# Nucleus step 0 with four threshold evaluations and a middle first point, open rows handled tile by tile, and the preparing stage folded into attention

## What is computed

```python
h = maximum(layernorm(x), 0)
x = x + L0(h, adj)        # eight-head graph attention, logits plus 2 * adj, zeros of adj masked
h = maximum(layernorm(x), 0)
x = x + L1(h, adj)        # diffusion and a nucleus-limited attention, two steps
...
# inside L1, for each of two steps:
logits = (Xa @ W1) @ W2 @ (Xa @ W3).T
vals = sort(logits, descending); csum = cumsum(softmax(vals))
k_i = sum(csum < 0.9) + 1                 # per row: smallest set of columns with 0.9 of the mass
A = softmax(where(rank < k_i, logits, -inf))
Xf = Rf @ Xf; Xb = Rb @ Xb; Xa = A @ Xa   # Rf, Rb: adj + 1 on the diagonal, divided by row or column sums
Z = Z + Xf @ U1[s] + Xb @ U2[s] + Xa @ U3[s]
```

## Time and profile before

| | us |
|---|---|
| median of three runs (3515.78 to 3516.79) | 3516.76 |
| the profiled execution | 3525.11 |
| its span, first to last instruction | 3523.3 |
| PE busy | 2934.2 |
| DVE busy | 2265.8 |
| ACT busy | 1292.9 |
| POOL busy | 50.1 |

### The profile page before, as it was taken

How to read it: one execution, slowest core, us unless ns; L and a number is a source line. 1 busy time by engine, 2 the same in 40 slices (tenths; PEclk the granted TensorE clock), 3 DMA queues, 4 the chain that set the end, 5 groups by cost and what they waited for, 6 DMA issues and landing times. The chain is left out here.

```text
span 3523.3 us, 57798 instructions
## 1 busy us (share of the span) xinstructions
PE 2934.2 (83%) x20374; PEld 2147.0 (61%) x20374; DVE 2265.8 (64%) x4452; ACT 1292.9 (37%) x1686; POOL 50.1 (1%) x68
## 2 busy tenths in 40 slices
PE   2469999999999999999999465887866568688599
PEld 1356666767667676676766244665645356577488
DVE  7955656556565655555556489789487987896430
ACT  4733434344334343434433221332414243422311
POOL 0000000000000000000000100000000000000110
PEclk7579999999999999999999787999988789899899
DMA  7937748386583865838568111101011000000500
GB/s 263 373 127 187 180 113 198 95 199 164 131 196 93 199 149 143 202 88 201 131 159 199 57 54 37 39 23 49 1 48 37 1 25 25 31 19 25 221 1 25
DMA packets 586123, 396.75 MB, mean 113 GB/s; under 512 B 538371, under 2 KB 551174, under 8 KB 560390
## 3 DMA queue, kind: packets, MB, share of 16 engines
q1 hardware_dynamic: 584262, 382.49, 39.8%
q10 hardware_dynamic: 1728, 12.58, 1.1%
HBM read 223.05 MB, written 37.75 MB: 74 GB/s over the span
## 5 line engine op out<-in xcount | busy, mean ns | idle before, releaser
L681 DVE SCALAR_TENSOR_TENSOR e_lo<-e,e_hi 128x2048 f16<-128x2048 f32 x128 | 293.3, 2291 | 448.1 <-ACT e_hi L606 448.1
L560 PE MATMUL av<-vw_hi,pT_hi 128*128 128x256 f16 x2048 | 559.4, 273 | 7.6 <-DMA pT_lo<-e_lo 7.6
L560 PE MATMUL av<-vw_lo,pT_hi 128*128 128x256 f16 x2048 | 559.4, 273 | 0.0
L560 PE MATMUL av<-vw_hi,pT_lo 128*128 128x256 f16 x2048 | 559.4, 273 | 0.0
L549 PE MATMUL logits<-kT_hi,qT_hi 128*128 128x512 f16 x1024 | 389.0, 380 | 7.2 <-DVE att_small L667 5.5
L1830 DVE SCALAR_TENSOR_TENSOR nuc_junk<-nuc_e,nuc_thr 128x2048 bf16<-128x2048 f32 x168 | 388.4, 2348 | 5.1 <-issue 0.5
L549 PE MATMUL logits<-kT_lo,qT_hi 128*128 128x512 f16 x1024 | 388.1, 379 | 0.0
L549 PE MATMUL logits<-kT_hi,qT_lo 128*128 128x512 f16 x1024 | 388.1, 379 | 0.0
L600 ACT ACTIVATE att_small<-att_small,minus 128x1 f32<-128x1 f32 x128 | 37.7, 295 | 829.2 <-DVE att_small L676 829.2
L667 DVE CUSTOM_DVE_ANT_0 e<-logits,bias,att_small 128x1024 f32<-128x1024 f32 x256 | 328.6, 1284 | 0.0
L601 ACT ACTIVATE e<-e,att_small,sc 128x2048 f32<-128x2048 f32 x128 | 266.2, 2079 | 0.0
(11 more groups left out here) (399 smaller groups left out, 5806.9 us busy)
## 6 DMA issues: line engine op xcount, KB each, us to landing
bias<-bias_scratch SPq DMA_DIRECT2D x130, 1024.0 KB, 4.8
bias_scratch<-adj_bias SPq DMA_DIRECT2D x16, 1024.0 KB, 8.0
adjT_scratch<-adjT SPq DMA_DIRECT2D x16, 1024.0 KB, 7.6
nuc_at_hi<-adjT_scratch SPq DMA_DIRECT2D x32, 512.0 KB, 3.9
nuc_at_lo<-adjT_scratch SPq DMA_DIRECT2D x32, 512.0 KB, 4.8
adjT<-adjT_scratch SPq DMA_DIRECT2D x16, 1024.0 KB, 19.5
adj_rows<-in_adj_dram ACTq DMA_DIRECT2D x12, 1024.0 KB, 9.2
adj_rows<-in_adj_dram SPq DMA_DIRECT2D x4, 1024.0 KB, 7.9
```

What stands on the lines that cost most here:

```text
L560: last = nc.tensor.matmul(AV[par][:, :], PT[par][w][:, m, :], VW[x][:, m, :], start=(m == 0 and w == x == 0), stop=(m == T - 1 and w == 1))
L681: nc.vector.scalar_tensor_tensor(out=EL[:, :], in0=E[par][:, :], scalar=P_SCALE, in1=EH[:, :], op0=ALU.mult, op1=ALU.subtract).then_inc(lo ...
```

## The change

- `CUTS` goes from (5, 7) to (4, 7). The first point, the clip and the aim become tables by step and evaluation: in step 0 the first point moves from 0.3 to 0.475 of the bracket, the clip from 0.1 to 0.01, 0.01, 0.2, the aim from 3 to 3, 4, 2. Step 1 keeps its values.
- In each group of step 0 the fifth `cut` is gone, and the row maxima of the group after next that stood between move into `look`.
- `look` of step 0 also hands over a flag for each tile, and `resolve` loops over the open tiles alone.
- `prepare` is gone. Its degree terms, weight maxima and scalars move to the start of `attend` (in scratch space inside `E[1]`), gamma and beta go through the two `AV` banks there, the beta sums and their stores move, tile by tile, behind the adds of the last head, and W1, W2, W3 are loaded at the start of step 0's `refresh`, where W3 is halved after the first centred tile.

```diff
-CUTS = (5, 7)
-FIRST_AT, CLIP = 0.3, 0.1
+CUTS = (4, 7)
+FIRST_AT = (0.475, 0.3)
+CLIP = ((0.01, 0.01, 0.2), (0.1,) * 6)
-AIM = 3.0
+AIM = ((3.0, 4.0, 2.0, 0.0), (3.0,) * 7)
...
-                phase(prepare, a, deg, scales, ident, ident16, halfp, w1, w2, w3, gb, sc, acc, Y, x_d, wtop)
...
+                def store(t):
+                    sp.wait_ge(shifted_s, t + 1)
+                    sp.dma_start(x_d[:, t, :], shifted[:, t % SHIFT_RING, :]).then_inc(x_stored[t % SHIFT_RING], 16)
...
+                        if t >= SHIFT_RING:
+                            store(t - SHIFT_RING)
...
                 bias(1, 1)
+                later_loads()
...
+                for par in range(SHIFT_RING):
+                    sp.wait_ge(x_stored[par], 16 * (T // SHIFT_RING + 1))
...
                 for n in range(3):
                     project(0, n)
+                pe.wait_ge(params_here, 32)
+                pe.wait_ge(vec, 1)
+                for n in range(2):
+                    last = nc.tensor.matmul(AV[n][:, :], ones, row[:, n * D:(n + 1) * D], start=True, stop=True)
+                last.then_inc(spread, 1)
...
+            @block.gpsimd
+            def _(pl):
+                pl.wait_ge(bases, 1)
+                for n in range(2):
+                    power = nc.gpsimd.tensor_tensor(scales[:, 2 + n, :], base[:, n, :], halfp[:, :], ALU.pow)
+                power.then_inc(powed, 1)
+                pl.wait_ge(ratios, 1)
+                nc.gpsimd.partition_all_reduce(top[:, 4:7], top[:, 0:3], P, ABSMAX).then_inc(largest, 1)
...
+                def weight_tops():
+                    v.wait_ge(raw_here, 32)
+                    for n in range(2):
+                        vlink.note(nc.vector.tensor_reduce(top[:, 4 + n:5 + n], raw[n], mybir.AxisListType.XY, ALU.max, apply_absolute_value=True))
...
+                    nc.vector.tensor_scalar(top[:, 1:3], top[:, 4:6], 1e-30, None, ALU.max).then_inc(ratios, 1)
+                    v.wait_ge(powed, 1)
...
+                def shift(i, t, par):
+                    v.wait_ge(av_free, i + 1 + AV_FREE)
+                    v.wait_ge(x_stored[par], 8 * (t - par) + 16)
+                    nc.vector.tensor_tensor(shifted[:, par, :], acc[:, ds(t, 1), :].rearrange("p a d -> p (a d)"), gb[:, 1, :],
+                                            ALU.add).then_inc(shifted_s, 1)
...
+                degree_terms()
                 weights(0)
                 for n in range(3):
                     evacuate(0, n)
+                gamma_beta()
...
                 evacuate(0, 3)
+                weight_tops()
                 lo(0, 0, link)
                 peaks(1, 1, 1, link)
                 masks(2, 0, link)
+                tops_apart()
...
                 add(T * HEADS - 2, T - 2, 0, link)
+                shift(T * HEADS - 2, T - 2, 0)
                 add(T * HEADS - 1, T - 1, 1, link)
...
+                shift(T * HEADS - 1, T - 1, 1)
...
+                        if t == 0:
+                            v.wait_ge(w_loaded, 16 * 5)
+                            nc.vector.tensor_scalar(w3[:, :, :, :], w3[:, :, :, :], 0.5, None, ALU.mult).then_inc(halved, 1)
...
-                    load(0)
+                    load(G)
                     with v.If(v.snap(left) > 0):
-                        settle(g, ALL)
-                        any_row(z_, 0)
-                        load(0)
-                        retry(g, ALL)
+                        for k in range(G):
+                            load(k)
+                            retry(g, slice(k, k + 1))
...
                     rest_parts(0)
                     peak(1, 2)
-                    cut(0, 4)
                     rest_parts(1)
                     rest_parts(2)
-                    look(0, lambda: peak(1, 3))
+                    look(0, {1: lambda: peak(1, 3)})
...
                     cut(1, 3)
                     peak(2, 1)
-                    cut(1, 4)
-                    peak(2, 2)
-                    look(1, lambda: peak(2, 3))
+                    look(1, {1: lambda: peak(2, 2), 3: lambda: peak(2, 3)})
```

## The result

| | before | after |
|---|---|---|
| median, us | 3516.28 (3513.11 to 3529.80, 8 executions) | 3504.44 (3503.16 to 3512.46, 8 executions) |
| profiled execution, us | 3525.11 | 3503.85 |
| its span, us | 3523.3 | 3502.0 |
| PE, DVE, ACT, POOL busy, us | 2934.2, 2265.8, 1292.9, 50.1 | 2930.1, 2227.1, 1293.1, 51.1 |

The ratio of the medians is 0.9966 (0.9953 to 0.9978): 11.8 us faster, where 25.2 us were forecast, with 3491.6 us. The sign and the range held, the size missed by 13 us. One thing has to be known for all that follows: executions of one kernel differ by 10 to 17 us, and the mean granted clock of TensorE differs with them (of the kernel before 3513.2 us at 0.929, 3529.5 at 0.925). Of 109 executions of the kernel before 82 lie at 3512 to 3519 us and 27 at 3520 to 3530. Both of its profiles were of the long ones, so the spans differ by 21.3 us where the medians differ by 11.8.

A forecast was written before the change was run, and what follows sets the result against it. DVE was taken to bound step 0 up to group 0's release, PE's chain after it, and the preparing stage to lie wholly on the path. -18.4 - 6.8 = -25.2 gave 3491.6 us; own range 3485 to 3498, whole range 3485 to 3531.

The forecast's parts named there:

- Part 1: Preparing stage moved: gap from attention's last add to first statistics shrinks, saving 20.5 us; -18.4 net of costs.
- What the moved work meets in attention: Attention: the moved instructions mostly stand where engines idle and cost nothing; only the weight maxima cost, 1.8 us.
- The weight maxima: Before attention's first `lo`, with no idle time to cover them: cost 1.8 us (1.5 to 2.5).
- lock rival: GpSimd's two powers beside `weights(0)` hold DVE under a shared port lock: 3494.5 us for one, 3497.4 for both; chance 0.12.
- Beta sums and stores: Attention's last head: one 0.45 us sum per item, where DVE idles for ACT; cost nothing, bound +4.
- The term put at nothing: Attention: beta sums and stores in the last head put at "Cost nothing"; other moved work under idle time also nothing.
- Part 2: Step 0 of the nucleus: four evaluations instead of five remove 47.4 us of DVE, of which 6.8 count.
- Group 0: Step 0, first release: DVE's maximum of tile 7 and all after it come 6.8 us earlier, 11.85 if waits dissolve.
- Groups 1 to 3: Later groups of step 0: worth 0, as PE arrives after DVE's release, 2.2 us late at group 1, 33.3 at group 2.
- the sign that the prediction called wrong: Forecast wrong if PE waits for the release of group 1, or if L1948 runs over 32 times.
- No open tile: Step 0's search: no row stays open after four evaluations; first open tile would cost 21 us, each further 17.
- The sum against the median: Sum of -25.2 us taken off the median 3516.76, which lies 8.35 below the profiled execution: 3491.6.

The follow-up runs named there:

- before_fill: Kernel before plus six unread transposes on TensorE in each refresh of step 0, filling its idle gaps: 3516.15 us, ratio 0.9996.
- prep_a10_fill: Kernel before with only the preparing stage moved, ten memsets on VectorE ahead of attention's loops, six unread transposes per step 0 refresh: 3495.62 us, ratio 0.9944.
- before_a25: Kernel before plus 25 one-column memsets on VectorE ahead of attention's loops: 3525.64 us, ratio 1.0026.
- before_a24: Kernel before plus 24 one-column memsets on VectorE ahead of attention's loops: 3523.67 us, ratio 1.0012.
- cuts_only: Kernel before with only step 0 of the nucleus changed (four evaluations, new constants), preparing stage left in place: 3513.51 us, ratio 0.9995.
- after_a10: Changed kernel plus ten one-column memsets on VectorE ahead of attention's loops: 3491.17 us, ratio 0.9929.
- prep_a10: Kernel before with only the preparing stage moved, plus ten memsets on VectorE ahead of attention's loops: 3505.57 us, ratio 0.9961.
- a10_fill: Changed kernel plus ten memsets on VectorE ahead of attention's loops and six unread transposes on TensorE per step 0 refresh: 3490.72 us, ratio 0.9932.
- prep_only: Kernel before with only the preparing stage moved, nucleus as before: 3504.32 us, ratio 0.9971.
- prep_n10: Kernel before with only the preparing stage moved, plus ten memsets on VectorE at the start of the nucleus: 3501.74 us, ratio 0.9955.
- after_fill: Changed kernel plus six unread transposes on TensorE in each refresh of step 0, filling its idle gaps: 3498.04 us, ratio 0.9953.

## Why the prediction was right, and where it was wrong

- *Part 1, the gap at the preparing stage.* Forecast 24.3 to 3.8, measured 3.36. With PE's gaps filled and without the gap in the loop, before_fill to prep_a10_fill, part 1 is worth 20.5 us (3516.15 to 3495.62, known to some 4 us) against 18.4.
- *What the moved work meets in attention.* The weight maxima cost 1.5 us, from 265.31 to 266.80, for 1.8 forecast; the evacuations ahead of them came 0.9 earlier and the first `e_lo` 0.6 later. The delay of the lock rival did not come, but the lock itself wasn't tested: DVE and GpSimd of after show that the sum with two SBUF operands was over before the powers began, with its old 0.75 us.

```profile
208.69 0.75 DVE L760 SCALAR_TENSOR_TENSOR wo_lo<-wo_stage,winv,wo_hi 128x512 f16<-128x512 f32 x1 [1.08 <-ACT wo_hi L668]
211.94 5.84 POOL L642 TENSOR_TENSOR scales<-e,halfp 128x16 f32<-128x16 f32 x2 [174.13 <-issue]
```

  The two powers, 5.84 us together, began 2.5 us after its end, beside evacuations, which read one operand from PSUM, and these took their 0.69 as in before. Beta sums and stores cost nothing: the last head's items take 10.54 us in both.
- *The term put at nothing.* This is the first step that failed. "Cost nothing" was right for every moved instruction and wrong for the loop behind them: moved code costs through the place of the code that follows it. 4.8 us over seven heads in after (0.09 us for each of 49 pairs make 4.4 of it), 4.9 in before_a25 against before_a24, both from the first `e_lo` to the last. It covers the 3.9 us that the two profiles miss, 21.3 us between them for the 25.2 forecast.
- *Part 2.* Group 0: forecast 6.8, in the traces 6.3 (cuts_only against before, and after_a10 against prep_a10), from the first maximum to the release. Groups 1 to 3 nothing in after, as forecast. But the 2.2 us by which PE was late at group 1 are thin: in after_a10 the jump ahead of that release costs 3.52 us instead of 1.07, with a transfer of instructions in it, and PE does wait, the sign that the prediction called wrong. PE of after_a10:

```profile
2281.87 0.82 PE L1570 MATMUL nuc_l<-ident,nuc_e 128*128 128x128 f32 x4 [2.08 <-DVE nuc_small L2115]
```

  By medians with the gaps filled part 2 is worth 4.9 (3495.62 to 3490.72), five executions each, so known to some 5 us. No open tile, as taken; one would have cost some 15.
- *The sum against the median.* This is the second step that failed, and the larger. The 8.35 us between the profiled execution and the median of before were carried over as a constant, as if after had the same distance; its profiled execution lies 0.6 us below its median. The clock's fall in step 0 fits this gap. Both long profiles of before have it, with 91.6 and 95.3 us in the stretch after the release of group 2; before_fill's, at 3515.25 us near the median of before, has not, and its stretch is 6.8 us shorter. Both profiles of after have it (91.5 and 92.0 us), at 3503.85 and 3506.47 among the bulk of its executions. No short execution of before was profiled, so that these lack the fall is inferred.
- *Together.* Without the fall and the gap in the loop after would be where the forecast had it: after_a10 is at 3491.17. Its profile is 12.1 us shorter than that of after: 6.3 in the stretch after the release of group 2, 4.9 in the loop, less 1.4 ahead of the first `e_lo` (memsets and what stands there), and 2.4 in small pieces. before_fill to a10_fill, the change is worth 25.4 us (21 to 27 by the spread of the executions) for 25.2 forecast. That this is so close is partly luck: part 1 gave 2.1 more and part 2 1.9 less than forecast.

Open stays which small shift decides whether an execution gets the fall, and why most executions of before_a24 are long. What delays DVE in the loop is known by its place alone. How much of after's missing 13 us belongs to each of the two steps is known from single profiles.

## What to carry to other kernels

Where code moves within an engine's stream, look at the loops behind it: compare the time per iteration, and shift them by a few idle instructions before believing a difference of a few tenths of a per cent. Before a forecast is set against a median, ask in which state of the clock the profiled execution was, stretch by stretch; where TensorE works in bursts with an engine between, harmless transposes in the gaps can buy the clock, as they did in prep_a10 and after. The best version here, the changed kernel with ten memsets, is at 3491.2 us (ratio 0.9929), with the transposes 3490.7 and a smaller spread.

## What the hardware showed that was not expected

- One instruction more ahead of a loop on VectorE made each pass of it 0.09 us longer, with no instructions fetched meanwhile (before_a24, before_a25).
- The same jump over unused code cost 0.26 to 0.55 us (prep_only), or 2.50 to 2.78 with one transfer of instructions in the gap (prep_n10), by where it stands.
- TensorE busy for three quarters of the time, with gaps of at most 1 us, was granted 0.71 (after); with six more transposes in each round it was granted 1.00 (after_fill), and the kernel was faster in the median by doing more. Without them, with like gaps, after_a10 was granted 1.00 too.
